# Local transformer: remainder gates and units in one block, and no work on masked zero columns

## What is computed

```python
# DIM = 256, HEADS = 16, DIM_HEAD = 64, WINDOW = 64, DIM_INNER = int(256 * 4 * 2 / 3) = 682
def local_attention(q, k, v):          # windows of 64 queries look at their own and the previous window
    mask = (it < jb) | (it > jb + w) | (jb == -1)
    sim = jnp.einsum('bhwie,bhwje->bhwij', bq, bk2) * QK_SCALE
    sim = jnp.where(mask, -jnp.finfo(sim.dtype).max, sim)
    attn = jax.nn.softmax(sim, -1)
    out = jnp.einsum('bhwij,bhwje->bhwie', attn, bv2)

def ffn_layer(x, g, bln, W1, b1, W2, b2):
    xn = (x - mu) / jnp.sqrt(var + 1e-05) * g + bln
    hg = xn @ W1 + b1                  # 256 -> 2 * 682
    a, gate = jnp.split(hg, 2, -1)     # units and gates
    return a * jax.nn.gelu(gate, approximate=False) @ W2 + b2
```

## Time and profile before

| | |
|---|---|
| median of 3 runs | 4340.77 us (4335.85 to 4342.06) |
| span of the profiled execution | 4357.8 us |
| TensorE, products busy | 3998.4 us, 92% |
| DVE, ACT, POOL busy | 3011.4, 2806.9, 1811.5 us |
| local stage (about 1240 to 2907 us) | 1667 us |

### The profile page before, as it was taken

The page is one execution under the profiler, slowest core; times in us unless marked ns, Lnnn a source line. Parts: engine busy times, 40 slices in busy tenths (PEclk is TensorE's granted clock), DMA queues, the critical chain, the costliest instruction groups (busy, mean ns, idle before and its releaser), DMA issues. The chain is left out here.

```text
span 4357.8 us, 81373 instructions
## 1 busy us (share of the span) xinstructions
PE 3998.4 (92%) x30320; PEld 2853.4 (65%) x30320; DVE 3011.4 (69%) x6897; ACT 2806.9 (64%) x5769; POOL 1811.5 (42%) x1862
## 2 busy tenths in 40 slices
PE   4999999988979999999999999967999999976998
PEld 3555555545757787887888888854555555535777
DVE  4777777767777767767677676644787877767745
ACT  2777777677967767777676776723676767654322
POOL 3333333204556555555556555523322322202644
PEclk7999999999989999999999999988999999988999
DMA  6666665536020110010100101027666666512265
GB/s 167 119 118 118 115 110 114 103 50 217 1 78 5 35 35 28 25 37 26 37 25 25 37 25 39 13 54 154 115 114 113 115 113 112 99 27 72 85 191 186
DMA packets 208194, 354.02 MB, mean 81 GB/s; under 512 B 26927, under 2 KB 110564, under 8 KB 205745
## 3 DMA queue, kind: packets, MB, share of 16 engines
q1 hardware_dynamic: 200217, 338.42, 35.4%
q0 software_dynamic: 7584, 10.39, 0.7%
HBM read 257.48 MB, written 114.98 MB: 85 GB/s over the span
## 5 line engine op out<-in xcount | busy, mean ns | idle before, releaser
L759 DVE TENSOR_REDUCE xa_m_part<-xa_unit 128x2 f32<-128x1024 f32 x1024 | 1247.7, 1224 | 515.3 <-PE xa_unit L907 513.8
L683 ACT ACTIVATE xa_ex<-xa_unit 128x1024 f32<-128x1024 f32 x1024 | 1029.8, 1019 | 259.7 <-PE xa_unit L891 254.4
L921 PE MATMUL xa_pv<-xa_ex,xa_vs 128*17 128x256 f32 x8192 | 546.5, 383 | 7.1 <-ACT xa_ex L683 7.0
L907 PE MATMUL xa_unit<-xa_ks,xa_q_base 48*128 48x512 f32 x2048 | 437.9, 425 | 117.8 <-ACT xa_ex L683 85.8
L1068 POOL TENSOR_SCALAR lt_p<-lt_p,lt_stat 128x192 f32<-128x192 f32 x384 | 355.3, 926 | 453.6 <-DVE lt_stat L1058 453.0
L891 PEld LDWEIGHTS xa_unit<-xa_q_base,xa_ks 50*128 50x128 f32 x4096 | 312.1, 185 | 316.2 <-issue 242.5
L891 PE MATMUL xa_unit<-xa_q_base,xa_ks 50*128 50x256 f32 x4096 | 502.5, 324 | 10.2 <-DVE xa_m_part L759 6.1
L1911 PE MATMUL lt_bank<-lt_wp,lt_xt 128*128 128x512 f32 x1728 | 465.1, 411 | 14.3 <-DVE lt_wp L1748 6.3
L1078 ACT ACTIVATE lt_p<-lt_p,lt_stat 128x128 f32<-128x128 f32 (+1 forms) x768 | 321.7, 420 | 157.2 <-DVE lt_stat L1053 154.5
L1911 PEld LDWEIGHTS lt_bank<-lt_wp,lt_xt 128*128 128x128 f32 x1728 | 314.5, 192 | 78.8 <-DVE lt_xt L1741 9.1
L618 POOL TENSOR_SCALAR xa_m_neg<-xa_m_blk 128x8 f32<-128x8 f32 x128 | 29.9, 233 | 780.4 <-DVE xa_m_blk L770 780.4
(11 more groups left out here) (334 smaller groups left out, 7903.3 us busy)
## 6 DMA issues: line engine op xcount, KB each, us to landing
xa_ks<-keys SPq DMA_DIRECT2D x372, 256.0 KB
keys<-xa_kp SPq DMA_DIRECT2D x128, 512.0 KB, 3.3
xa_cx<-in_ctx_t SPq DMA_DIRECT2D x64, 512.0 KB
lt_u<-in_lt_wqkv SPq DMA_DIRECT2D x54, 256.0 KB
places<-in_moe_blank SPq DMA_DIRECT2D x47, 258.0 KB, 8.6
moe_xs<-places SPq DMA_DIRECT2D x47, 258.0 KB
lt_w<-in_lt_w SPq DMA_DIRECT2D x6, 1536.0 KB
xa_q_base<-xa_m_rows SPq DMA_DIRECT2D x512, 2.0 KB
```

Of the source, the lines that this page charges most:

```text
L683: act.activation(x.ex[:, n % x.NE, :, :], x.place_of[step][:, :, :].rearrange("p o (j s) -> p (o j) s", j=2), ACT.Exp).then_inc(*x.ex_done ...
L759: dve.tensor_reduce(x.m_part[:, i % 2, qt, 2 * pair:2 * pair + 2, ch:ch + 1], x.place_of[step][:, :, :], AX.X, ALU.max).then_inc(*x.dve_ou ...
L907: mm = pe.matmul(bank[:, odd, :], x.q_base[rows, pair, b * S + qt * P:b * S + (qt + 1) * P], x.ks[unit % x.NU][rows, pair % 4, ch * 512:(c ...
L921: mm = pe.matmul(x.pv[32 * j:32 * j + x.VW, 0:S], x.vs[:, i % x.NV, kt, 4 * g + j, :], x.ex[:, n % x.NE, 2 * (j % 2) + j // 2, :], start=( ...
```

## The change

The blocks of the first feed-forward product are five full ones for gates and units each, and one that holds the remainders of both: gates in its columns 0..41, units in 64..105. The step "w1" 5 has one product over 256 columns with two parts of the contraction instead of two; gelu reads partitions 0..41 and writes 64..105, DVE works on partitions 64..105. `W2`'s last rows are laid out to match, with zeros in the others.

In a turn, the middle transposition reads only queries 128..191 and yields 64 columns, so `self.pt` has 320 columns and ACT copies 320. In an apply, keys 0..127 are multiplied with 192 columns, and keys 128..255 with 64 columns that are added to those and 64 columns that begin anew. For the conv attention, where `skip` is 0, all stays as it was.

```diff
--- before.py
+++ after.py
@@ -978,8 +978,15 @@
         self.keys, self.first, self.off = (P, 2 * P - skip), (0, skip), (0, P)
         self.place = (0, P + skip)
         self.width, self.n_pt, self.step = sum(self.keys), n_pt, P // at_once
+        shared, end = 2 * P - skip, 3 * P - skip
+        self.turned = ((P, slice(0, P)), (P - skip, slice(P, shared)), (P, slice(shared, end)))
+        self.weighed = ((True, False, slice(0, shared), slice(0, shared), 0),
+                        (False, True, slice(P, shared), slice(shared, shared + P - skip), 1))
+        if skip:
+            self.weighed += (True, True, slice(shared, 2 * P), slice(shared + P - skip, end), 1),
+        self.turned_width = end
         self.p = ctx.enter_context(nc.sbuf_tensor(f"{name}_p", [P, 5, 3 * P], F32))
-        self.pt = ctx.enter_context(nc.sbuf_tensor(f"{name}_pt", [P, n_pt, 3 * P], F32))
+        self.pt = ctx.enter_context(nc.sbuf_tensor(f"{name}_pt", [P, n_pt, 3 * P - skip], F32))
         self.stat = ctx.enter_context(nc.sbuf_tensor(f"{name}_stat", [P, 5, 4, 2], F32))
         f = c.flow
         self.s_full, self.low_done, self.exp_done = f("at_s_full"), f("at_low_done"), f("at_exp_done")
@@ -1021,9 +1028,9 @@
             on.wait_ge(self.div_dve, 2 * n + 2)
             on.wait_ge(self.div_pool, n + 1)
             on.wait_ge(self.t_out, n - 1)
-            for i in range(3):
-                at = slice(i * P, (i + 1) * P)
-                tr = pe.transpose(self.t_banks[n % 2][:, at], self.p[:, n % 5, at], self.c.ident[:, :])
+            for i, (queries, at) in enumerate(self.turned):
+                tr = pe.transpose(self.t_banks[n % 2][:, at], self.p[0:queries, n % 5, i * P:(i + 1) * P],
+                                  self.c.ident[0:queries, 0:queries])
             tr.then_inc(*self.t_full.one())
         elif kind == "apply":
             heads, call = h, n // self.at_once
@@ -1031,13 +1038,12 @@
             on.wait_ge(self.t_out, n + len(heads))
             if round_ == 0:
                 on.wait_ge(self.o_out, call // self.rounds)
-            for first, cols, keys, kt in ((True, slice(0, 2 * P), slice(0, 2 * P), 0),
-                                          (False, slice(P, 2 * P), slice(2 * P, 3 * P), 1)):
+            for begins, ends, cols, keys, kt in self.weighed:
                 for j, head in enumerate(heads):
                     mm = pe.matmul(self.o_bank[self.step * j:self.step * j + self.step, cols],
                                    st.v_of(b, kt, head), self.pt[:, (n + j) % self.n_pt, keys],
-                                   start=first and round_ == 0,
-                                   stop=not first and round_ == self.rounds - 1)
+                                   start=begins and round_ == 0,
+                                   stop=ends and round_ == self.rounds - 1)
             mm.then_inc(*self.pv_done.one())
 
     def dve_step(self, dve, on, st, step):
@@ -1081,7 +1087,7 @@
             on.wait_ge(self.t_full, n + 1)
             if n >= self.n_pt:
                 on.wait_ge(self.pv_done, (n - self.n_pt) // self.at_once + 1)
-            act.activation(self.pt[:, n % self.n_pt, :], self.t_banks[n % 2][:, 0:3 * P],
+            act.activation(self.pt[:, n % self.n_pt, :], self.t_banks[n % 2][:, 0:self.turned_width],
                            ACT.Copy).then_inc(*self.t_out.one())
         elif kind == "apply":
             call = n // self.at_once
@@ -1360,6 +1366,9 @@
 FF = int(D * 4 * 2 / 3)
 FC = -(-FF // P)
 FFP = FC * P
+FW = FC - 1
+FT = FF - FW * P
+W1 = (2 * FW + 1) * P
 
 
 class Local(Stage):
@@ -1397,7 +1406,7 @@
             def sb(n, shape, dt=F32):
                 return ctx.enter_context(nc.sbuf_tensor(f"lt_{n}", shape, dt))
             self.wp = sb("wp", [P, 2, 3, KC, INNER], F32R)
-            self.wo, self.w1, self.w2 = sb("wo", [P, HP, D]), sb("w1", [P, KC, 2 * FFP]), sb("w2", [P, FC, D])
+            self.wo, self.w1, self.w2 = sb("wo", [P, HP, D]), sb("w1", [P, KC, W1]), sb("w2", [P, FC, D])
             self.scl, self.rot = sb("scl", [P, 4, LH]), sb("rot", [P, 4, 2, LH])
             self.tab = sb("tab", [P, 4, 2, LH])
             self.b2 = sb("b2", [P, D])
@@ -1536,6 +1545,10 @@
 
         n = self.use[step]
         return self.gen_free[n % 3], n // 3 + 1
+
+    def gated_rows(self, m):
+
+        return (slice(0, P), slice(0, P)) if m < FW else (slice(0, FT), slice(64, 64 + FT))
 
     def y_wait(self, on, l, b):
 
@@ -1716,8 +1729,9 @@
                     if n >= 2:
                         lb, mo = divmod(n - 2, FC)
                         on.wait_ge(*self.freed(("w1", *divmod(lb, B), mo)))
-                    act.activation(self.gl[:, n % 2, :], self.bank(("w1", l, b, m))[:, S:2 * S], ACT.Gelu,
-                                   bias=self.ffc[:, l, 1, m:m + 1]).then_inc(*self.gelu_done.one())
+                    gates, units = self.gated_rows(m)
+                    act.activation(self.gl[units, n % 2, :], self.bank(("w1", l, b, m))[gates, S:2 * S], ACT.Gelu,
+                                   bias=self.ffc[gates, l, 1, m:m + 1]).then_inc(*self.gelu_done.one())
 
     def dve(self, dve):
         c, on, y = self.c, Waits(dve), self.c.x
@@ -1866,8 +1880,10 @@
                 for m in (mc, mc + 1):
                     n, at = FC * j + m, ("w1", l, b, m)
                     on.wait_ge(self.gelu_done, n + 1)
-                    dve.scalar_tensor_tensor(self.u[:, m, :], self.bank(at)[:, 0:S],
-                                             self.ffc[:, l, 0, m:m + 1], self.gl[:, n % 2, :], ALU.add,
+                    _, units = self.gated_rows(m)
+                    cols = slice(0, S) if m < FW else slice(S, 2 * S)
+                    dve.scalar_tensor_tensor(self.u[units, m, :], self.bank(at)[units, cols],
+                                             self.ffc[units, l, 0, m:m + 1], self.gl[units, n % 2, :], ALU.add,
                                              ALU.mult).then_inc(*self.freed(at)[0].one())
             elif kind == "fetched":
                 b, = a
@@ -1993,10 +2009,10 @@
                 m, = a[2:]
                 on.wait_ge(*self.freed(("ft", l, b)))
                 on.wait_ge(self.wb_in[1], l + 1)
-                for gate in (1, 0):
+                for gate in ((1, 0) if m < FW else (1,)):
+                    at = (gate * FW + m) * P if m < FW else 2 * FW * P
                     for k in range(KC):
-                        mm = pe.matmul(bank[:, gate * S:(gate + 1) * S],
-                                       self.w1[:, k, gate * FFP + m * P:gate * FFP + (m + 1) * P],
+                        mm = pe.matmul(bank[:, gate * S:(gate + 1) * S], self.w1[:, k, at:at + P],
                                        self.ft[:, k, :], start=(k == 0), stop=(k == KC - 1))
                 mm.then_inc(*self.gen_full.one())
             elif kind == "w2":
@@ -3017,14 +3033,22 @@
     f = np.float32
     o["lt_wqkv"] = a["L0_ffn_Wqkv"]
     o["lt_wo"] = a["L0_ffn_Wo"]
-    w1 = np.zeros((DEPTH, D, 2, FFP), f)
-    w1[..., :FF] = a["L0_ffn_W1"].reshape(DEPTH, D, 2, FF)
-    o["lt_w1"] = w1.reshape(DEPTH, D, 2 * FFP)
+    full = FW * P
+    both = a["L0_ffn_W1"].reshape(DEPTH, D, 2, FF)
+    w1 = np.zeros((DEPTH, D, W1), f)
+    w1[..., :2 * full] = both[..., :full].reshape(DEPTH, D, 2 * full)
+    w1[..., 2 * full:2 * full + FT] = both[..., 1, full:]
+    w1[..., 2 * full + 64:2 * full + 64 + FT] = both[..., 0, full:]
+    o["lt_w1"] = w1
     w2 = np.zeros((DEPTH, FFP, D), f)
-    w2[:, :FF] = a["L0_ffn_W2"]
+    w2[:, :full] = a["L0_ffn_W2"][:, :full]
+    w2[:, full + 64:full + 64 + FT] = a["L0_ffn_W2"][:, full:]
     o["lt_w2"] = w2
-    b1 = np.zeros((DEPTH, 2, FFP), f)
-    b1[..., :FF] = a["L0_ffn_b1"].reshape(DEPTH, 2, FF)
+    pair = a["L0_ffn_b1"].reshape(DEPTH, 2, FF)
+    b1 = np.zeros((DEPTH, 2, FC, P), f)
+    b1[:, :, :FW] = pair[..., :full].reshape(DEPTH, 2, FW, P)
+    b1[:, 1, FW, :FT] = pair[:, 1, full:]
+    b1[:, :, FW, 64:64 + FT] = pair[..., full:]
     o["lt_ffc"] = np.ascontiguousarray(b1.reshape(-1, P).T)
     ln = np.stack([a["L0_ffn_ln_g"], a["L0_ffn_ln_b"]], 1)
     o["lt_lnc"] = np.ascontiguousarray(ln.reshape(-1, P).T)
```

## The result

The changed kernel takes 4378.5 us (4374.8 to 4381.6, 4 runs) against 4339.1 for the kernel before on the same chips: ratio 1.0095, 95% interval 1.0081 to 1.0110, so 39 us **slower**.

The account below looks back on a forecast made before the run. TensorE's instructions, start to start, were taken to bound the local stage. +92 (64-row transposition) - 15.4 (value products) - 20.7 (feed-forward) = +56, less 4 of waits, +52: 4393 us from 4340.8; own range 4370 to 4432, 8-in-10 range 4290 to 4432.

Parts of the forecast that it names:

- The bound: Local transformer stage: time is what TensorE's instructions cost from start to start; layer forecast to grow from 269.1 to 277-279 us.
- The sign in the weight loads: Turn's three transpositions: TensorE's weight loads idle some 0.17 us ahead of the second and the third.
- Feed-forward block: First feed-forward product, last block: 4 instructions of 0.216 us fewer per job, 20.7 us less; bounds 17 to 20.7.
- ScalarE's copy at nothing: Copy of 320 columns instead of 384: 58 ns less each, 22 us of ScalarE, but no gain in kernel time.
- Short value products: Value product: 64-column pairs at 0.06 us, 0.08 us less a call, 15.4 us less; bounds 19 less to 23 more.
- The rival with 0.109: Value product: 64-column pairs follow each other no faster than 0.109 us, short products gain nothing; 4431 us, chance 0.08.
- The 64-row transposition: Middle transposition of each head: array shape changes there and back, 0.29 - 0.05 = 0.24 us more, 384 times, 92 us more.
- The row that spoke against it: Cross-attention: 8-column transposition, then full 128, shows no loss; supported the no-shape-change rival, 4291 us, chance 0.19.
- the one for waits that get used up: TensorE's waits ahead of the first feed-forward product: later arrival by 0.16 us uses up some 4 us of them.

Follow-up runs that it names:

- c1_after: The changed kernel, unaltered, run and profiled again on one chip with the kernel before: 4380.0 us, ratio 1.0096 to the kernel before.
- e1: Only the changed feed-forward block, with the attention of the kernel before: 4343.0 us beside 4359.0, ratio 0.9960.
- e3: The changed kernel with its middle transposition reading 96 rows and yielding 96 columns instead of 64: 4328.0 us, ratio 0.9925.
- e6: The changed kernel with its middle transposition reading 72 rows and yielding 72 columns instead of 64: 4298.4 us, ratio 0.9911, the fastest.
- c2_before: The kernel before, unaltered, profiled again on the same chip as c1_after: local stage 1670.7 us against 1710.1.
- e7: The kernel before with the middle full transposition of each local-stage head issued twice, 42 us of work added: ratio 1.0083, 36 us slower.
- e8: The kernel before with three more full transpositions for each local-stage head, 126 us of work added: ratio 1.0228, 99 us slower.
- e5: The changed kernel with the 64-row transposition issued ahead of the two full ones: 4358.2 us, ratio 1.0047.
- e2: The changed kernel with its middle transposition back at 128 rows and 128 columns, all else kept: 4327.3 us, ratio 0.9926.
- after (first profile): The changed kernel's first profile, taken at a different time from the profile before: local stage 1712.5 us against 1668.4.
- e4: The changed kernel with its 64-row transposition issued twice in a row: 4419.4 us, ratio 1.0140.

## Why the prediction was right, point by point

- **The bound.** TensorE's instructions, start to start, were the time of the stage. The layers bear it out: 269.1 us before, 276.4 in c1_after, with DVE, ScalarE and GpSimd busy as long as before to 0.4 us, or less (DVE 188.0, ScalarE 191.4, GpSimd 155.7 us a layer). I had 277 to 279. The sign in the weight loads, 0.17 us idle ahead of the second and of the third, came out as 0.22 (0.12 behind a value product) and 0.07: I had the sum of the starts right and not how the loads lie in it.
- **Feed-forward block.** 20.7 us forecast for the group, 20.1 measured. Whether all of it reached the end is open: e1 has 16 us, with an interval of 11 to 23.
- **ScalarE's copy at nothing.** Its mean fell from 478 to 424 ns, by 54 where I had put 58. Nothing shows that it was worth anything, and nothing that it wasn't: no run isolates it.
- **Short value products.** 15.4 us forecast, 18.1 measured. A pair of 64 columns follows the one before in 0.058 us by the starts in the trace (I took 0.06), and the next group starts 0.152 us after the last product instead of 0.203, the difference being the shorter product itself. The rival with 0.109 is gone.
- **The 64-row transposition.** 0.24 us more for each, 92 us, forecast; 91.3 measured. The starts are the ones written down for the half of the turns that follow the scores: 0.20, 0.20, 0.40 from first to last. In the other half the first distance is 0.26, for which the kernel before has 0.165, and the loss is the same. The row that spoke against it, L936's 8 columns, was rightly set aside: with 96 and 72 rows (e3, e6) there is no loss, with 64 there is, and L936 has 128. The Trainium skill, "TensorEngine Tiling (Array Packing)", When to Use Tiling, takes 64 rows or fewer for row tiling, and the runs agree. What it says there of few weight columns needn't bear on L936: by the page's Restrictions, column tiling disables the transpose mode for f32 input, and the 0.22 us for L936's two instructions agree with that.
- **The term that was off** is the one for waits that get used up. The three groups sum to +53.1; the stage grew by 39.4, so 13.7 us were absorbed where I had 4. I counted only the waits ahead of the feed-forward product, at 0.16 us a job; those went from 7.6 us (c2_before, 1440 to 2840 us) to 6.2. Of the 13.7, 5.9 us are beyond 0.45 us and 7.8 in shorter distances of other groups, above all the projections (3.9), the key transpositions (2.3) and the scores of `lt_q_odd` (1.8). Some 3 us of them are no waits at all but falls of the granted clock in c2_before that c1_after doesn't have (last section), and in the first pair of profiles only 9 us of the 53.1 are missing. So the term is 9 to 14 us by the profiles, and by the interval of the ratio (35 to 48 us slower) 5 to 18. e7 and e8 put such a loss at 6 us for 42 and 27 for 126; 91 us more in the same place lies between them. Whether it depends on the place of the added work or only on its sum is open.
- **4393 forecast, 4378.5 measured.** 52 us became 39; absorption accounts for 10 of the difference in the profiles of c1 and c2, and the value products for 3. Both terms were off in the same direction, so no error hid another.

The Trainium skill, "TensorE: Matmul & The Clock Gate", LDWEIGHTS, charges a weight load by its columns, which makes 107 ns for the 128 of a transposition. This case's trace doesn't agree: e6 shows the next transposition 0.066 us after one of 72 columns. In that group each weight load begins 0.002 us after the start of the product ahead of it, so the load of a transposition's 128 weight columns fits into that; 107 ns hold here for the plain products of the earlier trace rows, which are 0.107 us apart.

## What to carry to other kernels

Before cutting rows off a product or a transposition, look at what runs on both sides of it: in this dense stream two changes of the array's shape cost some 0.29 us, more than any single instruction of this stage saves by being shorter (the longest, a projection's 512 columns, takes 0.25 us). Cutting columns of the moving operand is free of this (the value products, 0.058 us for a pair of 64), and so is cutting rows down to 72, the fewest above 64 that were run: with 72 rows this kernel became 0.9% faster, with 64 rows 0.95% slower. Where the shape must change, place the instruction next to another change. And expect less than the sum of TensorE's instructions promises, even at 96% busy: of 53 us added 39 arrived, of 126 us 99. For work taken away no run here is clear of noise.

## What the runs showed of the hardware that I had not expected

The granted clock fell behind many of the waits of some 2 us. Each layer has one wait for DVE's L1805. Two layers of the kernel before (c2_before), then two of c1_after, two of e6 and two of e5, in the columns of the earlier trace rows:

```profile
1727.80:1997.70 269.90, 265.58 (x1576) 221.39 (x1576) 187.66 (x642) 194.16 (x513) 155.49 (x125) 0.99 0.10 30
1997.70:2266.80 269.10, 264.22 (x1576) 219.89 (x1576) 187.67 (x642) 194.14 (x513) 155.49 (x125) 1.00 0.10 30
```

```profile
1737.50:2014.00 276.50, 273.02 (x1689) 221.76 (x1689) 188.05 (x642) 191.53 (x514) 155.81 (x125) 1.00 0.09 29
2014.00:2290.40 276.40, 272.92 (x1688) 221.67 (x1689) 188.03 (x642) 191.43 (x513) 155.66 (x125) 1.00 0.09 29
```

```profile
1713.90:1976.50 262.60, 256.94 (x1688) 219.18 (x1689) 187.30 (x642) 191.00 (x513) 155.39 (x125) 0.99 0.10 31
1976.50:2239.30 262.80, 256.92 (x1689) 219.20 (x1689) 187.34 (x642) 191.17 (x514) 155.51 (x125) 0.99 0.10 31
```

```profile
1734.60:2007.70 273.10, 269.84 (x1689) 221.56 (x1689) 186.74 (x642) 191.55 (x513) 155.65 (x125) 0.99 0.10 29
2007.70:2280.80 273.10, 269.92 (x1689) 221.62 (x1690) 186.75 (x642) 191.62 (x514) 155.71 (x125) 0.99 0.09 30
```

Behind that wait the clock fell from its upper to its lower level (2.4 to 1.2 GHz) in four of five such layers of c2_before, where TensorE stood idle 2.2 us (in two of five in the first profile of that kernel), in all five of e6, at 2.2, and in none of c1_after, where it stood 1.96. That looks like a matter of the wait's length, but the other runs speak against it:

| run | idle before, us | layers with a fall, of 5 |
|---|---|---|
| e1 | 2.2 | 4 |
| e2 | 2.2 | 2 |
| e3 | 2.2 | 1 |
| e7 | 2.1 | 4 |
| e5 | 1.97 to 1.99 | 5 |
| after (first profile) | 1.96 to 2.00 | 1 |
| c1_after | 1.95 to 1.98 | 0 |
| e4 | 1.73 | 0 |
| e8 | 1.43 | 0 |

With 1.95 to 2.25 us idle it fell in none to all of the layers, in both profiles of one kernel differently; with 1.73 and less it never did. What decides in between is open. In the kernel before a layer with the fall lasts 0.8 us longer than one without. So c2_before's stage holds some 3 us of falls that c1_after's doesn't, and without them the stages would differ by some 3 us more than 39.4.
